# A mixture-of-experts decoder layer: the expert loop on TensorE flattened, weights split during the up projection, last token scatters with buffers of their own

## The chip, the cores and the metric

The kernel runs on one core of a Trainium2 chip, as one launch. The time is device microseconds of that core; less is better. The engines are named as in the profile: PE is TensorE (PEld its weight loads), ACT is ScalarE, DVE is VectorE, POOL is GpSimd, SP is SyncE, which only issues transfers.

## The reference, cut to what matters

A layer over 2 x 2048 rows of 512 numbers: linear attention, cross attention, and then a feed-forward part made of eight experts. The change touches the feed-forward part and the routing of the last rows before it.

```python
logits = x @ Wg.T                               # 4096 rows, 8 experts
top_v, top_i = jax.lax.top_k(logits, K)         # K = 2 experts a row
gates = jax.nn.softmax(top_v, axis=-1)
...
keep = pos_f < cap                              # cap = 1280 rows an expert
exp_batches = jnp.zeros((E, cap, d), x.dtype).at[flat_e, pos_safe].set(x[tok], mode='drop')
h = jnp.einsum('ecd,edf->ecf', exp_batches, W1)      # 512 -> 2 x 1024
inp, gate = jnp.split(h, 2, axis=-1)
h = jax.nn.gelu(inp, approximate=False) * gate
exp_out = jnp.einsum('eci,eid->ecd', h, W2)          # 1024 -> 512
out = jax.ops.segment_sum(contrib, tok, num_segments=N)   # each row: its experts' outputs times its gates
```

## The kernel before, in words

**Precision.** Every large product is made of three matmuls, because each operand is kept as a high part and a low part: high times high, high times low, low times high (`three`, L959 to L965; so one product shows as L963, L964 and L965 in a profile). ACT writes the high part (a copy that rounds), DVE subtracts it from the original and writes the low part (`low`, L1384).

**Before the experts.** The 4096 rows go through attention in eight groups of 512. For each group DVE finds the two experts of each row and their slots. POOL then writes row numbers and gates into a table in memory, eight indirect transfers a group (`scatter`, L600 to L607, shown as L605). `pack_tokens` (L1702) prepares the addresses `dest` and the words `pack` for them. Since there is one `dest` and one `pack`, DVE first waits until all scatters of the group before have landed (L1704). For the last group the row numbers are sent first, the gates later (`scatter_last_gates`, L608); DVE goes on with `cross_out` (L1661) only after `pack_tokens`. When all row numbers have landed, SP loads the first expert's part of the table (L472), POOL gathers the first four tiles of 128 rows (L651), and PE turns them (L1283).

**The experts.** Each of the eight has as many rows as were routed to it, known only at run time. They are worked off in chunks of four, four and two tiles (`CHUNKS`). A chunk is, on PE: `up`, eight jobs j of 24 matmuls over as many columns as there are rows (512, 384 or 256; L963 to L965 with output `pg`); two tiles of the next chunk turned (L1321, output `pt`); `out_tile(0)`, 24 matmuls (output `pj`); two more tiles turned when the next chunk has four; `out_tile(1)`; and tiles 2 and 3, or for tiles without rows an `empty_tile`, one matmul that only moves the counters on. PE's code is a loop over the experts around a loop over three chunks (L1287, L1293). At each expert it loads four numbers from the table `meta` into registers (L1288 to L1291), and chunks without rows are skipped by a branch (L1340).

For job j ACT makes the gelu (`gl`, L916), DVE multiplies with the other half (`hp`, L1808), ACT writes its high part (`hg_hi`, L919), DVE the low part (`hg_lo`). PE begins job j+2 when `hp` of job j is done, since `pg` has two banks for each half. The turned rows go from `pt` to `xe_hi` (ACT, L896) and `xe_lo` (DVE). An output tile is scaled by the gates on ACT into one of two buffers `ost` (L943) and added to the output by POOL with an indirect transfer (L682); each add waits for the one before to land.

**Weights.** An expert's weights come in twelve pieces of 512 KB, through four buffers `stage` (SP, L489): eight of the first matrix, four of the second. ACT copies a piece to its high part (`split`, L851, shown as L856), DVE writes the low part. The pieces of the second matrix are split within jobs 2 to 5 of the expert's first chunk. The eight pieces of the next expert's first matrix are split after the last chunk's `up`, on ACT between the output tiles (L935 to L938), on DVE after everything else (L1830 to L1832).

The order of all this is written out by hand; waits are on semaphores that count jobs, tiles and pieces.

## Time and profile before

| | |
|---|---|
| time, median of 3 runs | 1552.33 us (1551.38 to 1553.34) |
| the profiled execution's own time | 1546.13 us |
| its span, first to last instruction | 1544.3 us |
| PE busy | 1443.1 us, 93% of the span |
| DVE, ACT, POOL busy | 631.1, 586.0, 370.3 us |
| mean granted TensorE clock | 0.969 |
| PE's share of the chain that ended last | 80% |

A matmul's end is modelled: matmuls of 512 columns that start 0.23 us apart are shown as 0.39 us long each. So a stretch of PE is best read from the start of one instruction to the start of another. "Issue" as a releaser means that the engine waited for nothing that the profile shows: here register work and branches on its own sequencer.

### The profile page before, as it was taken

Reading aid. Unit: us, or ns where it says so; the run is one execution under the profiler, and the core shown is the slowest. Engines: PE = TensorE matmul, PEld = TensorE weight load, DVE = VectorE, ACT = ScalarE, POOL = GpSimd, SP = SyncE. Lnnn points to the kernel's source line nnn. Section 1 sums busy time; section 2 is a strip of 40 time slices with the busy share of each in tenths; the row PEclk is TensorE's granted clock in tenths of the full one; section 3 lists DMA queues with packets and bytes.
Section 4 is the critical chain, followed back from the end, with each engine's and each line's share of the span. In section 5 each row is a group of like instructions: output and inputs, shape, how many; then the busy total and the mean of one; then the engine's idle time right before and its main releaser. Section 6 shows DMA issues by size and latency. Waiting matters only on the chain.

```text
span 1544.3 us, 21052 instructions
## 1 busy us (share of the span) xinstructions
PE 1443.1 (93%) x7294; PEld 1208.9 (78%) x7295; DVE 631.1 (41%) x1410; ACT 586.0 (38%) x1001; POOL 370.3 (24%) x368
## 2 busy tenths in 40 slices
PE   6999999999983599999999899999999999999998
PEld 4768777778861487888888788898789888897886
DVE  6635666487775243311342431215441431214211
ACT  4535544367764142312332431234431422224211
POOL 3202222146765302011112112021112112021011
PEclk9999999999985699999999999999999999999999
DMA  9300220237655426221343432026523432035122
GB/s 204 56 0 28 82 110 28 82 102 200 164 120 144 124 79 165 60 34 21 96 143 54 129 89 41 7 48 190 148 83 54 113 104 41 0 54 150 14 41 27
DMA packets 80677, 132.46 MB, mean 86 GB/s; under 512 B 31954, under 2 KB 32082, under 8 KB 79604
## 3 DMA queue, kind: packets, MB, share of 16 engines
q1 hardware_dynamic: 63956, 97.67, 22.5%
q0 software_dynamic: 16672, 34.16, 12.0%
q8 instruction: 28, 0.46, 0.1%
q14 instruction: 21, 0.17, 0.0%
HBM read 93.90 MB, written 37.91 MB: 85 GB/s over the span
## 4 chain that ended last, share of the span: by engine, by line
PE 80%; POOL 4%; issue 4%; DVE 4%; DMA 4%; ACT 3%; ACTq 0%; SPq 0%; DVEq 0%; POOLq 0%
PE pg L963 16%; PE pg L965 15%; PE pg L964 15%; PE pj L963 8%; PE pj L965 8%; PE pj L964 8%; POOL slot_table L605 3%; PE pt L1321 1%; PE pj L1198 1%; DVE w_lo L1384 1%; DMA stage<-w 1%; DMA slot_table<-pack,dest 1%; PE pg L1226 1%; PE pg L1164 1%; DMA out_rows<-ost,etab 1%
## 5 line engine op out<-in xcount | busy, mean ns | idle before, releaser
L963 PE MATMUL pg<-xe_hi,w_hi 128*128 128x512 f32 (+2 forms) x1088 | 394.6, 363 | 21.9 <-issue 12.7
L965 PE MATMUL pg<-xe_hi,w_lo 128*128 128x512 f32 (+2 forms) x1088 | 393.3, 361 | 0.0
L964 PE MATMUL pg<-xe_lo,w_hi 128*128 128x512 f32 (+2 forms) x1088 | 393.2, 361 | 0.0
L1808 DVE TENSOR_TENSOR hp<-gl,pg 128x512 f32<-128x512 f32 (+1 forms) x136 | 87.1, 641 | 605.8 <-ACT gl L916 605.8
L682 POOL DMA_INDIRECT out_rows<-ost,etab x62 | 99.1, 1599 | 783.5 <-ACT ost L943 399.1
L963 PEld LDWEIGHTS pg<-xe_hi,w_hi 128*128 128x128 f32 x1088 | 207.8, 191 | 53.7 <-issue 14.2
L916 ACT ACTIVATE gl<-pg 128x512 f32<-128x512 f32 (+1 forms) x136 | 76.1, 560 | 456.3 <-PE pg L965 456.3
L965 PEld LDWEIGHTS pg<-xe_hi,w_lo 128*128 128x128 f32 x1088 | 207.7, 191 | 28.6
L964 PEld LDWEIGHTS pg<-xe_lo,w_hi 128*128 128x128 f32 x1088 | 207.9, 191 | 28.3
L963 PE MATMUL pj<-w_hi,hg_hi 128*128 128x512 f32 x464 | 183.4, 395 | 0.0
L965 PE MATMUL pj<-w_hi,hg_lo 128*128 128x512 f32 x464 | 180.8, 390 | 0.0
L964 PE MATMUL pj<-w_lo,hg_hi 128*128 128x512 f32 x464 | 180.7, 389 | 0.0
L1384 DVE TENSOR_TENSOR w_lo<-stage,w_hi 128x1024 fp32r<-128x1024 f32 x96 | 115.0, 1223 | 35.9 <-ACT w_hi L856 35.5
L943 ACT ACTIVATE ost<-pj,etab 128x512 f32<-128x512 f32 x62 | 42.6, 687 | 197.5 <-PE pj L965 186.8
L856 ACT ACTIVATE w_hi<-stage 128x1024 fp32r<-128x1024 f32 x96 | 99.0, 1057 | 40.0 <-DMA stage<-w 40.0
L965 PEld LDWEIGHTS pj<-w_hi,hg_lo 128*128 128x128 f32 x464 | 87.1, 188 | 18.3
L964 PEld LDWEIGHTS pj<-w_lo,hg_hi 128*128 128x128 f32 x464 | 87.2, 188 | 17.1
L963 PEld LDWEIGHTS pj<-w_hi,hg_hi 128*128 128x128 f32 x464 | 87.2, 188 | 17.1
L1384 DVE TENSOR_TENSOR hg_lo<-hp,hg_hi 128x512 fp32r<-128x512 f32 (+1 forms) x136 | 86.9, 639 | 1.9 <-ACT hg_hi L919 0.2
L919 ACT ACTIVATE hg_hi<-hp 128x512 fp32r<-128x512 f32 (+1 forms) x136 | 79.9, 587 | 4.1 <-DVE hp L1808 4.1
L605 POOL DMA_INDIRECT slot_table<-pack,dest x64 | 65.4, 1021 | 28.0 <-issue 17.2
L1384 DVE TENSOR_TENSOR xe_lo<-pt,xe_hi 128x512 fp32r<-128x512 f32 x66 | 42.6, 685 | 62.3 <-ACT xe_hi L896 62.1
(235 smaller groups left out, 1970.7 us busy)
## 6 DMA issues: line engine op xcount, KB each, us to landing
stage<-w SPq DMA_DIRECT2D x96, 512.0 KB, 5.0
xr<-x SPq DMA_DIRECT2D x8, 1024.0 KB, 10.0
out_rows<-xr SPq DMA_DIRECT2D x8, 1024.0 KB, 7.4
x_rows<-xn SPq DMA_DIRECT2D x8, 1024.0 KB, 7.4
x_in<-x SPq DMA_DIRECT2D x7, 1024.0 KB, 5.1
late_xT<-xT_hi SPq DMA_DIRECT2D x2, 1024.0 KB, 3.9
late_xT<-xT_lo SPq DMA_DIRECT2D x2, 1024.0 KB, 5.9
xT_hi<-late_xT SPq DMA_DIRECT2D x2, 1024.0 KB, 4.9
```

What stands on the lines that cost most here:

```text
L605: p.indirect_dma_start(out=to, out_offset=bass.IndirectOffsetOnAxis(ap=dest[:, c:c + 1], axis=0), in_=pack[:, c, 0:words], in_offset=None) ...
L682: p.indirect_dma_start(out=out, out_offset=bass.IndirectOffsetOnAxis(ap=etab[:, t, 0:1], axis=0), in_=ost[i % 2][:], in_offset=None, compu ...
L856: a.activation(w_dst(s), stage[s % STG][:], ACT.Copy).then_inc(s_w_hi, 1)
L916: a.activation(gl[j % 2][:, 0:w], pg[:, j % 2, 0:w], ACT.Gelu).then_inc(s_gl, 1)
L919: a.activation(hg_hi[:, j - 1, 0:w], hp[(j - 1) % 2][:, 0:w], ACT.Copy).then_inc(s_hghi, 1)
L943: a.activation(ost[i % 2][:], pj[i % 2][:], ACT.Copy, scale=etab[:, t, 1:2].bitcast(F32)).then_inc(s_yev, 1)
L963: nc.tensor.matmul(o, lh, rh, start=start, stop=False)
L964: nc.tensor.matmul(o, lh, rl, start=False, stop=False)
L965: return nc.tensor.matmul(o, ll, rh, start=False, stop=stop)
L1164: ins = mm(pg[:, 2 * (i % 2) + q // 2, (q % 2) * PW:(q % 2 + 1) * PW], qT[g % EARLY][:, q, i * P:(i + 1) * P], kv[g // NG][:, q, :], start ...
L1384: return v.tensor_tensor(dst, src, hi.bitcast(F32), ALU.subtract)
L1808: v.tensor_tensor(hp[j % 2][:, 0:w], gl[j % 2][:, 0:w], pg[:, 2 + j % 2, 0:w], ALU.mult).then_inc(s_hp, 1)
```

## The change

1. **PE.** One loop over 24 steps in place of the two loops. Six registers hold expert, chunk, rows left and three counters. The next values are worked out between `out_tile(0)` and `out_tile(1)`, with one load from `meta` for the next expert's count. Steps are not skipped in the middle; those left over come after the last chunk. An empty tile is now a matmul of 128 columns into `pg`, without a wait.
2. **ACT and DVE.** A loop over three chunks with one body in place of three written-out chunks. All operations are on 512 columns, also in chunks with fewer rows. Pieces of the second matrix are split in jobs 0 and 1 of an expert's first chunk, two each. The next expert's pieces are split in jobs 1 to 8 of its last chunk, one each, under an `If`.
3. **Output buffers.** Four `ost` in place of two; only tiles 0 and 1 wait for earlier adds.
4. **Last group.** `pack_last_tokens` writes `dest_tok` and `pack_last`, and waits for no scatter.

```diff
+            at_e, at_c, at_left, at_first, at_done, at_next = (
+                pe.alloc_register(f"pe_{n}") for n in ("expert", "chunk", "left", "first", "done", "count"))
...
-            with pe.Fori(0, EX) as e:
-                count = pe.value_load(meta[0:1, 0, bass.ds(e, 1)], min_val=0, max_val=CAP)
...
-                with pe.Fori(0, len(CHUNKS)) as c:
+            with pe.Fori(0, EX * len(CHUNKS)):
+                with pe.If(pe.snap(at_e, min_val=0, max_val=EX) < EX):
...
-                    def empty_tile(i):
-
-                        pe.wait_ge(s_yev, first + i)
-                        mm(pj[i % 2][:], w1_hi[:, 0, 0, 0:P], w2_hi[:, 0, :], start=True, stop=True).then_inc(s_y, 1)
+                    def empty_tiles(tiles):
+                        for i in tiles:
+                            mm(pg[:, 0, 0:P], hg_hi[:, 0, 0:P], w2_hi[:, 0, 0:P], start=True,
+                               stop=True).then_inc(s_y, 1)
...
+                    out_tile(0)
+                    pe.reg_load(at_next, meta[0:1, 0, bass.ds(e + 1, 1)])
...
+                    pe.reg_mov(at_left, (left - 4 * P) * more + coming * (more < 1))
+                    pe.reg_mov(at_e, e + (more < 1))
...
+                    out_tile(1)
```

ACT's new body (DVE's has the same frame, with `hp`, `hg_lo`, the low parts of pieces and `xe_lo`):

```diff
+                    weights_next = act.snap((left < 4 * P + 1) * (e < EX - 1), min_val=0, max_val=1)
...
+                        for j in range(FJ + 1):
+                            if j < FJ:
+                                act.wait_ge(s_h, done + (j + 1))
+                                if j >= 2:
+                                    act.wait_ge(s_hp, done + (j - 1))
+                                a.activation(gl[j % 2][:], pg[:, j % 2, :], ACT.Gelu).then_inc(s_gl, 1)
...
+                                a.activation(hg_hi[:, j - 1, :], hp[(j - 1) % 2][:], ACT.Copy).then_inc(s_hghi, 1)
+                            if j < 2:
+                                with act.If(c < 1):
+
+                                    act.wait_ge(s_y, first + 1)
+                                    for s in range(W1P + 2 * j, W1P + 2 * j + 2):
+                                        split(e, s)
+                            if j >= 1:
+                                with act.If(weights_next > 0):
+
+                                    split(e + 1, j - 1)
+                        evac(range(2))
+                        out_scaled(0)
+                        with act.If(next_is_full > 0):
+                            evac(range(2, 4))
+                        out_scaled(1)
+                        with act.If(c < 2):
+                            out_scaled(2)
+                            out_scaled(3)
```

The last group on DVE:

```diff
-                    pack_tokens(g)
+                    pack_last_tokens()
...
+            def pack_last_tokens():
+
+                link(v.tensor_tensor(slot[:], slot[:], trash[:], ALU.add))
+                flat = slot[:].rearrange("p i k -> p (i k)")
+                v.tensor_scalar(dest_tok[:], flat, 2.0, None, ALU.mult)
+                v.tensor_copy(pack_last[:, :, 0], tok[:].rearrange("p i k -> p (i k)")).then_inc(s_dest, 1)
```

PE before, at the head of the loop over the experts, ahead of the first `up` of an expert (ISA is a register operation):

```order
L1287 ISA
L1288 TENSOR_LOAD meta_125
L1288 ISA x2
L1289 ISA
L1289 TENSOR_LOAD meta_125
L1289 ISA x2
L1290 ISA
L1290 TENSOR_LOAD meta_125
L1290 ISA x2
L1291 ISA
L1291 TENSOR_LOAD meta_125
L1291 ISA x2
```

PE after: the head of its one loop, up to the first matmul of `up`.

```order
L1303 UNCONDITIONAL_BRANCH
L1304 COMPARE_AND_BRANCH
L1305 ISA
L1353 COMPARE_AND_BRANCH
L1315 ISA
L1317 ISA
L971 MATMUL pg<-xe_hi_206,w1_hi_196 128x512
```

PE after, between the last matmul of `out_tile(0)` and the first of `out_tile(1)`:

```order
L973 MATMUL pj0<-w2_hi_202,hg_lo_205 128x512
L1370 ISA
L1370 TENSOR_LOAD meta_127
L1372 COMPARE_AND_BRANCH
L1330 ISA
L1332 MATMUL pt0<-ident_49,xg_208 128x128 x4
L1330 REGISTER_ALU
L1332 MATMUL pt1<-ident_49,xg_208 128x128 x4
L1372 UNCONDITIONAL_BRANCH
L1374 ISA
L1376 ISA
L971 MATMUL pj1<-w2_hi_202,hg_hi_204 128x512
```

Four loads stood ahead of an expert's first matmul; now none does, and one load and the bookkeeping stand between the two output tiles of every chunk.

ACT before, after the last job of a third chunk: the high part of job 7, then the turned rows, then pieces.

```order
L919 ACTIVATE hg_hi_202<-hp1_210 128x256
L895 REGISTER_ALU
L896 ACTIVATE xe_hi_204<-pt0 128x4x128
L895 REGISTER_ALU
L896 ACTIVATE xe_hi_204<-pt1 128x4x128
L936 COMPARE_AND_BRANCH
L853 ISA
L856 ACTIVATE w1_hi_194<-stage0_196 128x1024
L856 ACTIVATE w1_hi_194<-stage1_197 128x1024
```

ACT after, job 7 and what follows it, for any chunk (the pieces only in an expert's last):

```order
L942 ACTIVATE gl1_210<-pg 128x512
L947 ACTIVATE hg_hi_204<-hp0_211 128x512
L955 COMPARE_AND_BRANCH
L857 ISA
L858 ACTIVATE w1_hi_196<-stage2_200 128x1024
L955 UNCONDITIONAL_BRANCH
L947 ACTIVATE hg_hi_204<-hp1_212 128x512
L955 COMPARE_AND_BRANCH
L857 ISA
L858 ACTIVATE w1_hi_196<-stage3_201 128x1024
L955 UNCONDITIONAL_BRANCH
```

The pieces have moved from behind the turned rows to ahead of them, one behind each job.

## Rows read from the trace of the kernel before

**Rows 1.** Windows: us, busy of PE, PEld, DVE, ACT, POOL; granted clock, DMA share, GB/s.
```profile
481.00:522.40 41.40, 6.25 (x19) 3.11 (x18) 15.67 (x41) 13.27 (x22) 19.14 (x22) 0.50 0.50 125
522.40:1536.30 1013.90, 994.54 (x4908) 849.84 (x4908) 307.84 (x422) 310.54 (x491) 165.35 (x134) 0.99 0.32 77
```
**Rows 2.** Waits of PE from 522 on: us in total, times, longest.
```profile
PE pg L963 <- issue: 12.7, 4, 5.1
PE pg L963 <- DVE w_lo L1384: 7.3, 4, 2.9
PE pg L963 <- DVE hp L1808: 1.9, 1, 1.9
```
**Rows 3.** Groups of PE by form from 522.3 on: busy, mean ns, idle before.
```profile
L963 PE MATMUL pg<-xe_hi,w_hi 128*128 128x512 f32 x704 | 279.1, 397 | 18.5 <-issue 12.7 <-DVE w_lo L1384 5.8
...
L963 PE MATMUL pj<-w_hi,hg_hi 128*128 128x512 f32 x464 | 183.4, 395 | 0.0
...
L963 PE MATMUL pg<-xe_hi,w_hi 128*128 128x256 f32 x256 | 72.5, 283 | 0.0
L963 PE MATMUL pg<-xe_hi,w_hi 128*128 128x384 f32 x128 | 43.0, 336 | 3.4 <-DVE hp L1808 1.9 <-DVE w_lo L1384 1.6
```
**Rows 4.** Windows of PE alone: one stretch each of `up` or output tiles.
```profile
663.68:707.21 43.53, 43.53 (x193) 1.00 0.10 21
708.00:729.86 21.86, 21.86 (x100) 1.00 0.25 30
729.86:752.89 23.03, 23.03 (x193) 1.00 0.29 65
1176.34:1209.65 33.31, 33.31 (x193) 1.00 0.18 42
522.40:568.64 46.24, 46.24 (x192) 0.94 0.38 115
594.88:640.14 45.26, 45.26 (x192) 0.96 0.34 91
876.89:923.35 46.46, 46.46 (x192) 0.94 0.44 125
```
**Rows 5.** Timeline of the last group's tokens: start, us, instruction, idle before.
```profile
488.41 0.17 DVE L1709 TENSOR_TENSOR slot<-slot,trash 128x8 f32<-128x8 f32 x1 [7.38 <-DMA slot_table<-pack,dest]
489.20 0.96 POOL L605 DMA_INDIRECT slot_table<-pack,dest  x1 [7.28 <-DVE pack L1713]
...
499.68 0.96 POOL L605 DMA_INDIRECT slot_table<-pack,dest  x1 [0.30 <-issue]
...
507.26 0.38 SPq L472 DMA_DIRECT2D etab_next<-slot_table  x1
```
**Rows 6.** Timeline of one job with a piece, and of the end of that `up`.
```profile
1073.82 0.60 ACT L916 ACTIVATE gl<-pg 128x512 f32<-128x512 f32 x1 [2.09 <-PE pg L965]
1074.84 1.06 ACT L856 ACTIVATE w_hi<-stage 128x1024 fp32r<-128x1024 f32 x1
1074.45 0.69 DVE L1808 TENSOR_TENSOR hp<-gl,pg 128x512 f32<-128x512 f32 x1 [1.47 <-ACT gl L916]
1075.92 1.23 DVE L1384 TENSOR_TENSOR w_lo<-stage,w_hi 128x1024 fp32r<-128x1024 f32 x1 [0.18 <-ACT w_hi L856]
1086.11 1.03 PE L1321 MATMUL pt<-ident,xg 128*128 128x128 f32 x8
1088.93 1.28 DVE L1384 TENSOR_TENSOR xe_lo<-pt,xe_hi 128x512 fp32r<-128x512 f32 x2
```
**Rows 7.** PE's sequencer, one line each: ns min/median/max, first and last start.
```profile
L1288 PEldq TENSOR_LOAD <-meta x8: 310/320/816, 518.3 to 1397.7; - x8
L1341 PEldq COMPARE_BRANCH  x28: 65/169/3335, 521.9 to 1508.9; - x28
```
**Rows 8.** ACT's waits from 522.4 on; landing of weight pieces from 600 on.
```profile
ACT L916 <- issue: 12.2, 8, 2.1
DMA to landing us min/median/max: 3.1/4.8/6.7
```

More of the change, by code:

```diff
@@ L256, in decoder @@
     hp = [ff(f"hp{i}", [P, GT]) for i in range(2)]
-    ost = [ff(f"ost{i}", [P, D]) for i in range(2)]
+    ost = [ff(f"ost{i}", [P, D]) for i in range(4)]
     assert base + ffn_at[0] <= nc.sbuf_usable_end, ffn_at
@@ L946, in _ @@
-                jobs(0)
-                with act.If(count > 4 * P):
-                    outs(0, False, CHUNKS[1])
-                    jobs(1)
-                    with act.If(count > 8 * P):
-                        outs(1, False, CHUNKS[2])
-                        jobs(2)
-                        outs(2, True, CHUNKS[0])
-                    with act.Else():
-                        outs(1, True, CHUNKS[0])
-                with act.Else():
-                    outs(0, True, CHUNKS[0])
+                three_chunks = act.value_load(meta[0:1, 3, bass.ds(e, 1)], min_val=0, max_val=1)
@@ new lines, in _ @@
+                    with pe.If(left > 3 * P):
+                        up(4)
+                    with pe.Else():
+                        with pe.If(left > 2 * P):
+                            up(3)
+                        with pe.Else():
+                            up(2)
+                    more = pe.snap(left > 4 * P, min_val=0, max_val=1)
+                    next_is_full = pe.snap((c % 2) * more < 1, min_val=0, max_val=1)
+                    gathered = pe.snap((first + (c < 2) * 2) * 16 + next_is_full * 32, min_val=32,
+                                       max_val=16 * (EX * ET + 16))
@@ L1361, in _ @@
+                    pe.reg_mov(at_e, e + (more < 1))
+                    pe.reg_mov(at_c, (c + 1) * more)
+                    pe.reg_mov(at_first, following)
+                    pe.reg_mov(at_done, done + FJ)
+                    out_tile(1)
+                    with pe.If(c < 2):
+                        with pe.If(left > 2 * P):
+                            out_tile(2)
                             with pe.If(left > 3 * P):
@@ L1363, in _ @@
                             with pe.Else():
-                                empty_tile(3)
+                                empty_tiles(range(3, 4))
+                        with pe.Else():
+                            empty_tiles(range(2, 4))
         @block.vector
```

212 lines of the change are left out of this document (93 added, 119 removed).

## The prediction

> **What bounds the kernel now.** I first read the windows by stage: from 522.4 to 1536.3 us, 1013.9 us long, PE does the experts and is busy for 994.5 us [rows 1]. So only what PE waits for, or does slowly, can be saved there, however much ACT and DVE gain. Ahead of it lie 41.4 us in which PE has 6.25 us of work at the low clock (0.50) while the last group is routed [rows 1].
>
> Second, the waits of PE [rows 2]. From 522 on it waits 12.7 us for "issue" in four places, 7.3 us for the low part of a weight piece in four, 1.9 us once for `hp`. One of the four "issue" waits is the start of the first expert; since the seven others for "issue" and `w_lo` are as many as there are changes of expert, I take the first matmul of each of the experts 1 to 7 to be what waits.
>
> Third, how long the stage takes without waits. The groups by form give the count: 704 matmuls of one line and 512 columns are 11 `up` of 64 each, 128 of 384 columns are 2, 256 of 256 columns are 4, and 464 are 58 output tiles of 8 [rows 3]. Undisturbed lengths are 43.53, 33.31 and 23.03 us for an `up` with 512, 384 and 256 columns, and 21.86 us for four output tiles, 5.465 each; between the end of one window at 707.21 and the next at 708.00 lie eight transposes, 0.79 [rows 4]. The sum is 11 x 43.53 + 2 x 33.31 + 4 x 23.03 + 58 x 5.465 + 34 x 0.79 = 478.8 + 66.6 + 92.1 + 317.0 + 26.9 = 981.4 us. Measured are 1013.9. So 32.5 us are lost.
>
> Where they go: the waits of rows 2, less some 3 us for the first start, are 18.7 us. After longer gaps the granted clock falls to the lower of its two levels for a few us: an `up` of 512 columns takes 45.26 after the first change and 46.46 at 876.89, with mean clock 0.96 and 0.94, against 43.53 at 1.00 [rows 4]. That is 1.7 and 2.9 us. Two more such gaps, by the waits of rows 2, I put at 1.7 each, so 8 us in all. The first `up` loses 46.24 - 43.53 = 2.7 us in the same way, after the 41 us of routing. The rest, 3 us, are the empty tiles and the part of each gap that the modelled ends of matmuls cover.
>
> **The change part by part.**
>
> *PE's loop.* Before, four loads from `meta` with their register operations stand ahead of an expert's first matmul. The first of them starts at 518.3 and the first matmul at 522.4; 1397.7 is the last [rows 7]. One load takes 0.32 us in the median, and with the operations around it I take 0.75, so 3 us for the four and over 4 with the loop's branches. All "issue" waits are this, less what PE still has queued. The `w_lo` waits are, I think, mostly this too, since ACT and DVE finish a piece at about the same time. Now six short instructions stand there, under 1 us. What is queued covers that: the one branch of 3.3 us in 28 [rows 7], within the first expert, is followed by no wait of PE in rows 2. Gain: the 18.7 - 1.9 us of gaps, the 8 us of low clock and 3 us of rest, 27.8, if the pieces are there.
>
> *Pieces during `up`.* They are: the first is split in job 1 of the last chunk, 20 us or more before the next expert. In this place the `w_lo` waits go whatever the register work was. The new cost is on ACT and DVE. One job with a piece keeps ACT from 1073.82 to 1074.84 + 1.06, 2.1 us, and DVE from 1074.45 to 1075.92 + 1.23, 2.7 us [rows 6]. A job of PE lasts 43.53 / 8 = 5.4, 4.2 or, in the narrow chunks, 2.9 us. So both keep up; DVE with only 0.2 us to spare in the four narrow ones, which are also charged the full 512 columns now. PE needs `hp` of job j one job later, and `hp` comes before the piece in DVE's order, so 0.2 us is not PE's margin; that is over 1 us. Cost 0.
>
> *The end of the last `up`.* Two pieces now stand ahead of `xe_lo` on DVE. Before, at the end of an `up` (PE turns at 1086.11), the two `xe_lo` end at 1088.93 + 1.28, 4.1 us later [rows 6]. Two pieces of 1.2 make that 6.5. PE wants it for the last four transposes after 0.79 + 5.47 + 0.4 = 6.65 us. Just in time, but then the bookkeeping (two register operations, some 0.3 us) is no longer covered. I take 0.5 us x 7 experts = 3.5; bounds 0 and 1.5 x 7 = 10.5, were DVE a further piece late.
>
> *The load and bookkeeping in each chunk.* Behind `out_tile(0)` a load of 0.3 to 0.8 us, in 17 chunks. 24 matmuls are queued or being queued there; cost 0, at most 0.8 x 17 = 13.6 if nothing covered it. I take 0.5.
>
> *One-chunk experts.* In their only chunk four pieces of the second matrix and eight of the next expert go through ACT, and the transfer of the next expert's first piece waits for the last adds and for a free buffer, then takes 4.8 us, 6.7 at most [rows 8]. ACT waits for it in job 1, in order, ahead of the next gelu. With jobs of 5.4 us it fits. With the 4.2 us of the expert at 1050 I expect up to 1 us; I take 0.5. The 1.9 us wait for `hp`, which is of this kind and in this expert, goes, since ACT is no longer held by pieces at the start.
>
> *Empty tiles and four output buffers.* The empty tile's wait for ACT is in the gaps already counted. ACT's waits for adds held no matmul but that.
>
> Stage of the experts: 27.8 + 1.9 - 3.5 - 0.5 - 0.5 = 25.2 us less.
>
> *Last group.* DVE waits 7.38 us for the scatters of group 6, and POOL 7.28 us for DVE; its usual spacing is 0.30 [rows 5]. With buffers of its own the wait is gone, and all behind it (scatters, the norm, `cross_out`, the store of the rows, the table load) moves up by 7.28 - 0.30 = 7.0 us. What comes last then? The last scatter is issued at 499.68, and the load that waits for its landing goes at 507.26 [rows 5]: over 6 us of landing under a megabyte of rows and two pieces of weights. These transfers move up with it, but now closer behind earlier ones. I take 6.5 us; bounds 7.2 and, if the table's writes are bound by transfers and not by DVE, 2. The low clock at the first `up` stays: PE still idles over 20 us.
>
> *Sum.* 25.2 + 6.5 = 31.7 us. The profiled execution, 1546.1 us, becomes 1514.4; the median of the runs lies 6.2 above it, so 1520.6.
>
> **A rule against this change.** There are over ten new conditional branches in every chunk on ACT and DVE. What the rows show of branches: 27 of 28 of L1341 take some 0.2 us or less, one takes 3.3, the first time it jumps far [rows 7]. The Trainium skill (Runtime: NRT & Kernel Launch, Instruction fetch mechanics) says that a taken branch to a target outside the code held on chip forces a fetch before anything goes on. By the rule each long jump would stall again and again; the trace agrees for the first jump and shows no second one, for PE. For ACT and DVE it is the slower rival below.
>
> **The rivals.**
> 1. *Late pieces (12%).* In the narrow last chunks a piece is wanted every 2.9 us. Four buffers and a cycle of 1.1 + 1.2 + 4.8 us allow one per 1.8; at a landing of 6.7 plus queueing behind gathers and adds, one per 3.5 or more. Then ACT waits in order ahead of gelu: 0.6 to 1 us x 8 jobs x 4 chunks = 20 to 30 us lost at worst, some 15 likely: 1535. For it: pieces do make ACT wait now. Against: four are loaded beforehand.
> 2. *The routing does not shorten (12%).* Scatters land late under the other transfers, gain 2 in place of 6.5: 1525.
> 3. *Register work not covered (10%).* After `out_tile(0)`, 0.8 us in each of 17 chunks, and 1.5 us at each last chunk: 13.6 + 7 more, 1541 at most, 1532 likely.
> 4. *Branches fetch code (4%), slower.* ACT's "issue" waits at the head of its expert loop are 12.2 us in 8, 1.5 each [rows 8]. If a taken branch cost that in each job, DVE's narrow jobs last 4.2 us in place of 2.9 (4 x 8 x 1.3 = 42 us) and each end of `up` is 1.5 to 3 us later (17 x 1.5 = 26): 68 us, 1588. It decides from some 0.6 us a branch on. Against: these waits hold several loads and a branch each.
>
> **How the numbers follow.** The forecast, 1520.6, has 62%; its own range is 1515 to 1528. The range of 8 in 10 reaches down to 1514, all costs at 0 and the full 7.2, and up into rivals 1 and 3, to 1533. A change of 0.2% (3 us) is about what the runs can tell. Only rival 4, or 1 and 3 together, come near no gain: faster 0.94, same 0.02, slower 0.04.
>
> **What would show it.** Right: PE's longest wait between experts under 0.5 us and none from `w_lo`; an `up` of 512 columns at 43.5 everywhere but in the first expert; the stage of experts at 986 to 991 us; the wait at DVE's slot addition gone and the first `up` at about 516. Wrong: narrow `up`s longer than 23.03; waits of `pt` for `xe_lo` over 1 us; ACT waiting for `stage` within `up`.

## The result: 38 us less, and more than was forecast

The changed kernel takes 1513.99 us in the median of its runs (1509.47 to 1517.61), the kernel before 1552.07 in the runs beside it. The ratio is 0.9749, with a 95% interval of 0.9731 to 0.9766. The forecast was 1520.6 us; its range began at 1514.0, and the median lies just below it.

The profiled execution took 1509.47 us with a span of 1507.8. Against the profiled execution of the kernel before this is 36.7 us less.

The windows of the changed kernel, cut at its first and last expert matmul, answer to [rows 1]. Columns as there.

```profile
477.00:516.64 39.64, 12.15 (x39) 5.67 (x40) 19.36 (x68) 13.48 (x23) 22.61 (x26) 0.50 0.66 160
516.64:1499.80 983.16, 983.16 (x4908) 843.67 (x4908) 319.50 (x422) 330.52 (x500) 168.13 (x135) 1.00 0.33 80
```

The experts take 983.2 us in place of 1013.9, so 30.7 less, and PE is busy in every one of them. The first `up` starts at 516.64 in place of 522.40, so 5.8 earlier. From the last matmul to the end it is 8.0 us in both. 30.7 + 5.8 + 0.2 outside the span are the 36.7.

PE's waits from 480 us on answer to [rows 2] (total, times, longest):

```profile
PE pt L1291 <- DMA xg<-x_rows,etab_next: 26.0, 4, 25.1
PE pg L971 <- issue: 1.5, 1, 1.5
```

Both lie ahead of the first expert matmul. Behind it none is left, where there were 18.7 us in eight (the 21.9 in nine of [rows 2] hold the start of the first expert, 3.2 us).

Groups of PE by form answer to [rows 3]: the work is the same, the idle time before it is 0.

```profile
L971 PE MATMUL pg<-xe_hi,w_hi 128*128 128x512 f32 x704 | 274.8, 390 | 1.5 <-issue 1.5
...
L971 PE MATMUL pg<-xe_hi,w_hi 128*128 128x256 f32 x256 | 72.4, 283 | 0.0
...
L971 PE MATMUL pg<-xe_hi,w_hi 128*128 128x384 f32 x128 | 42.8, 334 | 0.0
```

Windows of PE, one `up` each, answer to [rows 4]: the first, then one with 512 columns, one with 256, the first one behind a change of expert, and the one with 384 at the start of the expert that stood still for `hp` before.

```profile
516.64:561.74 45.10, 45.10 (x192) 0.97 0.55 180
585.37:628.90 43.53, 43.53 (x194) 1.00 0.29 82
718.65:741.69 23.04, 23.04 (x194) 1.00 0.64 170
754.36:797.88 43.52, 43.52 (x193) 1.00 0.27 79
1026.39:1059.70 33.31, 33.31 (x193) 1.00 0.57 182
```

The lengths are the undisturbed ones to 0.01 us, at the full clock (behind empty tiles an `up` of 512 columns takes 43.6). The narrow `up` of 23.04 us is one under which seven early pieces are split: it isn't longer. Only the first is, by 1.6 us.

The end of that narrow `up` in the timeline, PE and DVE, answers to [rows 6]:

```profile
741.69 1.03 PE L1332 MATMUL pt<-ident,xg 128*128 128x128 f32 x8
748.03 1.03 PE L1332 MATMUL pt<-ident,xg 128*128 128x128 f32 x8
```

```profile
743.98 1.22 DVE L1408 TENSOR_TENSOR w_lo<-stage,w_hi 128x1024 fp32r<-128x1024 f32 x1 [0.18 <-ACT w_hi L858]
745.13 0.68 DVE L1408 TENSOR_TENSOR hg_lo<-hp,hg_hi 128x512 fp32r<-128x512 f32 x1
745.73 1.22 DVE L1408 TENSOR_TENSOR w_lo<-stage,w_hi 128x1024 fp32r<-128x1024 f32 x1
746.86 1.28 DVE L1408 TENSOR_TENSOR xe_lo<-pt,xe_hi 128x512 fp32r<-128x512 f32 x2
```

PE turns the first pair at 741.69. `xe_lo` of both is done at 746.86 + 1.28 = 748.14, 6.45 us later. PE comes for the second pair at 748.03 and goes through it without a wait, because tile 2 needs only the first of the two, which is done 0.5 us before, and tile 3 comes a moment later: its first transpose starts 0.3 us after the second `xe_lo` is done.

The last group's tokens answer to [rows 5]: group 6's first scatter, then DVE's slot addition, the first and last scatter of the row numbers, the load of the table.

```profile
473.28 1.09 POOL L609 DMA_INDIRECT slot_table<-pack,dest  x1 [2.98 <-DVE pack L1747]
...
483.39 0.17 DVE L1739 TENSOR_TENSOR slot<-slot,trash 128x8 f32<-128x8 f32 x1
484.42 0.95 POOL L609 DMA_INDIRECT slot_table<-pack_last,dest_tok  x1 [0.30 <-issue]
...
494.90 0.96 POOL L609 DMA_INDIRECT slot_table<-pack_last,dest_tok  x1 [0.30 <-issue]
...
503.02 0.38 SPq L475 DMA_DIRECT2D etab_next<-slot_table  x1
```

The two waits of over 7 us are gone. In the kernel before, group 6's first scatter was at 471.10, so this execution came 2.2 us late to this place. Counted from it, the first `up` starts after 43.4 us in place of 51.3, which is 7.9 less.

ACT's waits from the first `up` on, of those in [rows 8]:

```profile
ACT ost L926 <- DMA out_rows<-ost,etab: 63.6, 14, 4.6
ACT L942 <- issue: 26.4, 8, 4.4
...
ACT w_hi L858 <- DMA stage<-w: 6.0, 6, 3.2
```

The waits for issue grew to 26.4 us from 12.2, and those for adds are 63.6 us. At the head of an expert ACT does register work: ahead of the gelu at 760.0, for one, four loads from `meta` of 0.27 to 0.28 us each stand with their operations from 755.4 to 757.8. All six waits for `stage` lie within an `up`, five in the first 20 us of the first one and one of 0.9 us in the expert that starts at 1026.4. None of it reaches PE.

### The profile page after: what moved, and what is told of

Its sections match the earlier page's. It is cut to its first block, busy times and chain, and to the rows that moved or that the text cites. A ratio compares the mean times of both kernels' runs of the same rounds, so it can differ in the third digit from the quotient of the medians.

```text
span 1507.8 us, 21734 instructions
## 1 busy us (share of the span) xinstructions
PE 1429.8 (95%) x7294; PEld 1201.5 (80%) x7295; DVE 643.3 (43%) x1410; ACT 605.5 (40%) x1010; POOL 372.4 (25%) x368
## 3 DMA queue, kind: packets, MB, share of 16 engines
q0 software_dynamic: 16672, 34.16, 12.4%
## 4 chain that ended last, share of the span: by engine, by line
PE 83%; POOL 4%; DMA 4%; DVE 3%; ACT 3%; issue 2%; SPq 0%; POOLq 0%; ACTq 0%; DVEq 0%
PE pg L971 16%; PE pg L973 16%; PE pg L972 16%; PE pj L971 9%; PE pj L973 9%; PE pj L972 9%; POOL slot_table L609 3%; PE pt L1332 2%; PE pj L1206 1%; DMA out_rows<-ost,etab 1%; PE pt L989 1%; DMA stage<-w 1%; PE pg L1172 1%; POOL qT L581 1%; PE pg L1234 1%
## 5 line engine op out<-in xcount | busy, mean ns | idle before, releaser
L971 PE MATMUL pg<-xe_hi,w_hi 128*128 128x512 f32 (+2 forms) x1088 | 390.0, 358 | 1.5 <-issue 1.5
L1844 DVE TENSOR_TENSOR hp<-gl,pg 128x512 f32<-128x512 f32 x136 | 93.5, 687 | 593.4 <-ACT gl L942 588.7
L942 ACT ACTIVATE gl<-pg 128x512 f32<-128x512 f32 x136 | 81.3, 598 | 375.9 <-PE pg L973 367.7
L1408 DVE TENSOR_TENSOR hg_lo<-hp,hg_hi 128x512 fp32r<-128x512 f32 x136 | 93.1, 685 | 1.0
L947 ACT ACTIVATE hg_hi<-hp 128x512 fp32r<-128x512 f32 x136 | 84.8, 624 | 2.3 <-DVE hp L1844 2.3
L609 POOL DMA_INDIRECT slot_table<-pack,dest x56 | 58.0, 1036 | 19.9 <-issue 15.2
## 6 DMA issues: line engine op xcount, KB each, us to landing
stage<-w SPq DMA_DIRECT2D x96, 512.0 KB
```

The costliest lines, as they stand in the source:

```text
L609: p.indirect_dma_start(out=to, out_offset=bass.IndirectOffsetOnAxis(ap=at[:, c:c + 1], axis=0), in_=words, in_offset=None).then_inc(s_scat ...
L942: a.activation(gl[j % 2][:], pg[:, j % 2, :], ACT.Gelu).then_inc(s_gl, 1)
L947: a.activation(hg_hi[:, j - 1, :], hp[(j - 1) % 2][:], ACT.Copy).then_inc(s_hghi, 1)
L971: nc.tensor.matmul(o, lh, rh, start=start, stop=False)
L1408: return v.tensor_tensor(dst, src, hi.bitcast(F32), ALU.subtract)
L1844: v.tensor_tensor(hp[j % 2][:], gl[j % 2][:], pg[:, 2 + j % 2, :], ALU.mult).then_inc(s_hp, 1)
```

## The experiments

Kernels of one round ran on one chip, with the kernel before beside them, and its median (in one round a single time) lay between 1544.6 and 1546.5 us there, 5.6 to 7.5 us lower than on the chip above. So I compare ratios, and apart from them the length of the experts' stage, which is read from one execution: from the first to the last expert matmul. It repeats well: the changed kernel has 983.2, 984.5, 983.8 and 983.9 us in four executions, while the start of the first `up` differs by 3 to 4 us between executions of the same kernel.

| kernel | time or ratio to the kernel before (95%) | experts' stage, us |
|---|---|---|
| last group alone | 0.9966 (0.9946 to 0.9987) | 1013.0 |
| PE's loop alone | 0.9880 (0.9863 to 0.9897) | 992.9 |
| ACT, DVE, four buffers alone | 0.9994 (0.9978 to 1.0010) | 1008.4 |
| changed kernel beside them | 0.9756 (0.9734 to 0.9777) | 984.5 |
| loads at the head, unused | one run, 1506.5 (before 1545.1) | 983.3 |
| loads in the middle, unused | one run, 1508.8 | 984.0 |
| one piece twice | one run, 1516.4 | 990.8 |
| two output buffers | one run, 1510.4 (before 1545.1) | 988.8 |
| four loads at the head | one run, 1528.9 (before 1545.7) | 1003.0 |
| five loads in the middle | one run, 1531.3 | 1005.5 |
| long filler | 0.9891 (0.9864 to 0.9918) | 992.6 |
| changed kernel beside it | 0.9767 (0.9738 to 0.9797) | 983.8 |
| short filler | 0.9769 (0.9746 to 0.9792) | 984.0 |
| changed kernel beside it | 0.9771 (0.9747 to 0.9795) | 983.9 |
| code moved | one run, 1518.3 (before 1546.5) | 991.8 |

### The parts one by one

**Last group alone.** The kernel before with `pack_last_tokens`:

```diff
-                    pack_tokens(g)
+                    pack_last_tokens()
```

> The kernel before with the fourth part of the change alone (own buffers for the last group's tokens). Theory A (the 7.0 us of waiting are the gain, transfers do not take any back): the first `up` starts 6.0 to 7.0 us earlier than 522.4, the four loads ahead of it and its low clock (46.2 us) stay, time 1552.1 - 6.5 = 1545.6, 1544.5 to 1546.5. Rival B (the table's writes are bound by transfers): gain 2, 1550.

Measured: the first `up` at 516.18, and 44.05 us after group 6's first scatter in place of 51.30. From that scatter to the last group's first one it takes 11.14 us in place of 18.10; in thirteen further executions with this edit it took 11.11 to 11.16. Theory A is right: the wait was worth 7.0, and nothing was taken back by the transfers: the landing behind the last scatter took 7.4 us, before 7.6. The ratio makes it 5.3 us of time, with an interval of 2 to 8.

**PE's loop alone.** ACT and DVE split the pieces where they did before, behind the turned rows.

```diff
-            with pe.Fori(0, EX) as e:
-                count = pe.value_load(meta[0:1, 0, bass.ds(e, 1)], min_val=0, max_val=CAP)
...
+            with pe.Fori(0, EX * len(CHUNKS)):
```

> The kernel before with TensorE's single loop and the new empty tiles alone; pieces are still split behind the turned rows and 522.4 us still stand ahead of the experts. Theory A (all gaps between experts, those put down to `w_lo` too, were register work): experts' stage 983 to 986 us from first to last `up` matmul start as in the changed kernel, no `w_lo` wait over 0.5 us, time 1552.1 - 31 = 1521, 1519 to 1524. Rival B (the `w_lo` waits were late pieces, so moving the pieces into `up` earned its share): four waits for `w_lo` of 1.5 to 3 us stay with 1.7 us of low clock behind each, 16 us saved at most, time 1534 to 1540.

Measured: ratio 0.988, 18.5 us, the stage 21.0 us shorter. Both theories are half wrong: A has the waits right, B is near the time. PE's waits behind the first `up`'s start in this kernel, one line in all:

```profile
PE pg L963 <- DVE hp L1824: 7.3, 4, 3.3
```

The pieces are split where they were before and PE comes sooner, yet there is no `w_lo` wait left: these were register work, as A says. But a wait that was not there before has come up: PE starts the new expert at once, does its first two jobs, and stands still for `hp` of job 0. DVE in the timeline around one such change of expert:

```profile
751.13 1.29 DVE L1400 TENSOR_TENSOR xe_lo<-pt,xe_hi 128x512 fp32r<-128x512 f32 x2 [4.57 <-ACT xe_hi L896]
752.33 4.62 DVE L1400 TENSOR_TENSOR w_lo<-stage,w_hi 128x1024 fp32r<-128x1024 f32 x4
...
762.49 2.46 DVE L1400 TENSOR_TENSOR w_lo<-stage,w_hi 128x1024 fp32r<-128x1024 f32 x2 [0.26 <-ACT w_hi L856]
767.23 1.28 DVE L1824 TENSOR_TENSOR hp<-gl,pg 128x512 f32<-128x512 f32 x2 [2.29 <-ACT gl L916]
```

The eight pieces keep DVE until 764.95 and ACT nearly as long, and only then come gelu and `hp` of job 0, which PE had ready at 761.4. Two windows of PE show what it costs, an `up` of 512 and one of 384 columns that should take 43.5 and 33.3 us:

```profile
755.97:800.79 44.82, 43.85 (x193) 1.00 0.52 168
1031.85:1070.27 38.42, 35.11 (x193) 0.96 0.61 195
```

In the second the clock fell too. Four such places make 10 us of the stage.

**ACT, DVE and four buffers alone.** PE's loops as before.

```diff
+                            if j >= 1:
+                                with act.If(weights_next > 0):
+
+                                    split(e + 1, j - 1)
```

> The kernel before with the loops of ScalarE and VectorE, the pieces within `up` and four output buffers alone; TensorE's loops as before. Theory A (register work is all): the gaps between experts stay at 1.5 to 5 us, all now put down to issue, time 1552.1 less 0 to 3 us, 1549 to 1552. Rival B (pieces were late): gaps halve, and 10 to 16 us go, 1536 to 1542. Rival C (branches or 512-column work on the other engines cost TensorE something that its own new loop hid): 1555 or more.

Measured: ratio 0.9994, no change that can be told, as theory A has it; the stage 5.5 us shorter. Of these 2.2 are at the expert whose `up` of 384 columns stood still for `hp` before (33.4 us in place of 35.6), 1.1 are a shorter low clock in the first `up` (45.1 us), and the rest is low clock behind gaps that stayed (one `up` of 43.6 us where it was 45.3, one of 45.7 where it was 46.5), so what the part itself earned is nearer to 2 us. PE's waits from the first `up`'s start on:

```profile
PE pg L969 <- issue: 20.1, 8, 5.5
PE pj L1344 <- ACT ost L924: 0.8, 1, 0.8
```

In [rows 2] 12.7 us were put down to issue and 7.3 to `w_lo`, 20.0 together in eight. Here, with every piece split well ahead, 20.1 in eight are all issue. So the `w_lo` waits named the wrong cause: the releaser that came last by the profile was DVE, but PE's sequencer was still at its registers.

**The changed kernel beside them.**

> The changed kernel once more, beside its parts: 1514, 1512 to 1517. If the parts add up (theory A: 6.5 + 31 + 0 = 37.5, less than 2 us from their meeting), it lies within 2 us of 1552.1 minus the sum of the three gains; if parts need each other (rival B), the three gains add up to 10 us less than its own.

The three gains are 5.3 + 18.5 + 0.9 = 24.7 us, its own is 37.7 us. Each of these is known to some 3 us, so the times speak for rival B: the parts need each other. The stage, which is less noisy, says that by 3 to 4 us they do: 21.0 + 5.5 = 26.5 us alone, 29.4 to 30.9 together. PE's loop uncovers 10 us of late pieces, and moving the pieces is worth little until it does. The other 9 of the 13 us are not found in the traces: the stage and the front of the parts alone (26.5, 7.0, and 1.5 from the four loads ahead of expert 0) make 35 us.

### The costs that I had charged

**One piece twice** (the eighth piece of an expert, into a scratch buffer first):

```diff
+                if again:
+                    low(scratch[:], stage[s % STG][:], hi)
                 low(lo, stage[s % STG][:], hi).then_inc(s_w_lo, 1)
```

> The changed kernel with the subtraction of an expert's eighth early piece done twice on VectorE (the first into a scratch buffer), which puts 1.1 to 1.2 us ahead of `xe_lo` at the end of each last `up`, 7 times. It measures the margin that I called just in time. Theory A (margin about 0.5 us, as 6.45 us from the turn to the end of the second `xe_lo` in the changed kernel's trace would have it): the second pair of turned tiles comes 0.5 to 0.9 us late in 7 chunks, 3.5 to 6.5 us more. Rival B (the margin is over 1.2 us): nothing. Rival C (none, and bookkeeping behind it uncovered): 1.2 to 2 us each, 8 to 14 us.

Measured: PE waits in seven places, one line in all from the first `up`'s start on; the stage is 990.8 us, 6.3 to 7.6 more.

```profile
PE pt L1333 <- DVE xe_lo L1409: 3.8, 7, 0.6
```

`out_tile(0)` and the second pair of turned tiles take 6.26 + 1.07 us there in place of 5.55 + 0.79, so 1.0 us in each place. From the first turn to the end of the second `xe_lo` it is 7.60 us in place of 6.45, so DVE was 1.15 us later. The margin is thus 0.15 us by this reckoning, 0.3 by the timeline above. The loss is just above A's 3.5 to 6.5 us, and "just in time" was right. The 0.5 us a place that I charged on top was not there in the changed kernel. Here it shows in part: where PE has to wait for `xe_lo`, the second pair takes 1.07 us in place of 0.79, so 0.3 us of bookkeeping behind it are no longer covered.

**Loads at the head and in the middle of a step, first attempt.**

```diff
+                    for _ in range(4):
+                        pe.reg_load(at_next, meta[0:1, 0, bass.ds(e + 1, 1)])
```

> The changed kernel with four extra loads from `meta` at the head of each chunk, ahead of `up`: the old register work put back, now in 17 chunks and with the pieces within `up`. Theory A (the sequencer's work costs only what exceeds the matmuls still queued): four loads of 0.3 to 0.75 us come on top of under 1 us, 2.3 to 4 us in all against a cover of 2.2 to 3.6, so gaps of 0 to 1.5 us at the start of `up`, 5 to 25 us in all over 17 chunks; all put down to issue, none to `w_lo`. Rival B (four loads alone are hidden; it was the nested loops and branches that made the gaps): no gap, no change. Rival C (nothing covers them): 17 x 3 = 50 us more.

> The changed kernel with four more loads behind `out_tile(0)` in each chunk, five in place of one. Theory A (24 matmuls and the turned tiles are queued there): no gap over 0.4 us between the output tiles, time unchanged within 2 us. Rival B (what I charged at up to 0.8 us a load is real and hidden by little): 1 to 3 us in each of 17 chunks, 17 to 50 us more.

Neither tells anything on these theories: nothing used the loaded values, and the traces have 17 + 1 loads of PE as in the changed kernel. They serve as two more executions of it, with stages of 983.3 and 984.0 us. So the loads were made live.

**Four loads at the head** (one behind `out_tile(0)` less):

```diff
+                    count = pe.value_load(meta[0:1, 0, bass.ds(e, 1)], min_val=0, max_val=CAP)
+                    tb = pe.value_load(meta[0:1, 1, bass.ds(e, 1)], min_val=0, max_val=EX * ET)
+                    ib = pe.value_load(meta[0:1, 2, bass.ds(e, 1)], min_val=0, max_val=EX * 3)
+                    three_chunks = pe.value_load(meta[0:1, 3, bass.ds(e, 1)], min_val=0, max_val=1)
+                    left = pe.snap(count - c * (4 * P), min_val=-8 * P, max_val=CAP)
```

> The changed kernel, but at the head of each step of its loop four numbers of the expert are loaded from `meta` and used (rows left, first tile, counter, three chunks), as the kernel before did once per expert; the load behind `out_tile(0)` is gone. In the first attempt at this, head_loads, nothing used the loaded values, no load is in its trace, and it tells nothing. Theory A (only what exceeds the queued matmuls costs): register work of 4 us against a cover of 2.2 to 3.6 leaves gaps of 1 to 2 us at 16 further starts of `up`, 16 to 32 us, and up to 1.7 us of low clock behind the longer ones: the experts' stage is 1005 to 1030 us in place of 983 to 984.5. Rival B (the two nested loops, not the loads, made the gaps): stage under 987. Rival C (nothing covers): 16 x 3.5 = 56, stage 1040.

Measured: the stage is 1003.0 us, 18.5 to 20 more, just below A. PE's only wait from the first `up`'s start on:

```profile
PE pg L971 <- issue: 15.5, 16, 1.5
```

**Five loads in the middle** (four live ones behind `out_tile(0)` more):

```diff
                     coming = pe.snap(at_next, min_val=0, max_val=CAP)
+                    tb = pe.value_load(meta[0:1, 1, bass.ds(e + 1, 1)], min_val=0, max_val=EX * ET)
+                    ib = pe.value_load(meta[0:1, 2, bass.ds(e + 1, 1)], min_val=0, max_val=EX * 3)
+                    none1 = pe.value_load(meta[0:1, 3, bass.ds(e, 1)], min_val=0, max_val=1)
+                    none2 = pe.value_load(meta[0:1, 3, bass.ds(e, 1)], min_val=0, max_val=1)
```

> The changed kernel with four more loads, whose values are used, behind the load that follows `out_tile(0)` in each chunk (in mid_loads they were unused and are not in its trace). Theory A (as at the head: the sequencer is some 2.2 us ahead of TensorE there, five loads with their operations take 4 us or more): a gap of 1 to 2 us before the turned tiles in 17 chunks, 17 to 35 us more, so that one load fits under the queue and five do not. Rival B (a whole output tile of 5.5 us covers them): time within 2 us of the changed kernel's, stage 983 to 985.

Measured: the stage is 1005.5 us, 21 to 22 more. A is right in the sum. PE's waits from the first `up`'s start on:

```profile
PE pt L1332 <- issue: 10.9, 14, 1.4
PE pj L971 <- ACT ost L926: 3.3, 3, 1.1
```

From start to start the loss is 1.9 us in the seven last chunks with an expert behind them (1.6 in the first of them), 1.4 in each of the three ahead of a narrow chunk, where no tiles are turned in between, and 0.6 in each of the others. PE in the timeline at one such place, and the operations of one of the five loads (ns min/median/max, first and last start):

```profile
1030.60 0.39 PE L973 MATMUL pj<-w_hi,hg_lo 128*128 128x512 f32 x1
1032.40 0.87 PE L1332 MATMUL pt<-ident,xg 128*128 128x128 f32 x6 [1.41 <-issue]
```

```profile
L1372 PEldq TENSOR_LOAD <-meta x17: 294/301/317, 566.9 to 1501.4; - x17
L1372 PEldq FUSED_REGOPS  x17: 159/159/159, 567.2 to 1501.7; - x17
L1372 PEldq SEQ_ASSERT  x17: 18/18/24, 567.5 to 1502.0; - x17
```

The load itself takes 0.30 us; with what stands around it the live ones follow each other every 0.7 to 0.8 us. Here the sequencer takes from 1028.8 to 1032.1, 3.3 us, for the five loads with their operations. Its first load begins 1.8 us before PE's last matmul of `out_tile(0)` starts. So about 2 us of sequencer work are covered at this place, one of those with the largest loss. One load and the bookkeeping fit under it, which is why they cost nothing in the changed kernel; by this reckoning, an estimate, about three loads are the limit.

**Two output buffers** in place of four:

```diff
-                        if i < 2:
-
-                            act.wait_ge(s_add, used if i == 0 else first * 16 + 16)
-                        a.activation(ost[i][:], pj[i % 2][:], ACT.Copy,
+                        act.wait_ge(s_add, used if i == 0 else first * 16 + 16 * i)
+                        a.activation(ost[i % 2][:], pj[i % 2][:], ACT.Copy,
```

> The changed kernel with two output buffers in place of four: ScalarE waits for an earlier add before each of the four scaled tiles. Theory A (the adds held no matmul): time unchanged within 2 us, ScalarE's waits for `out_rows` grow by 20 us or more, TensorE's do not. Rival B (with pieces in job 0 and 1 and gelus behind them, a late ScalarE reaches TensorE): waits of `pg` for `hp` or of `pj` for `ost` appear, 1 to 2 us in some of the four-tile chunks, 5 to 20 us more.

Measured in one execution: PE waits once for `hp`, 2.6 us, at the start of the fourth expert, behind a chunk with two tiles without rows. With the low clock behind it that `up` is long by 4.6 us (48.15 us from 853.81 on; the window holds the two empty tiles ahead of it too). ACT is what is late: it waits for an add until 860.43, and its first gelu of that `up` starts 12.4 us after the first matmul, in the changed kernel 6.3.

```profile
853.64:901.97 48.33, 45.70 (x196) 0.96 0.31 82
860.43 0.69 ACT L924 ACTIVATE ost<-pj,etab 128x512 f32<-128x512 f32 x1 [5.11 <-DMA out_rows<-ost,etab]
```

So B in one place, in one execution. Four buffers are worth up to 5 us there, in company with PE's new loop; I had put them at nothing.

### The low clock at the first `up`, and the code

**Long filler.** Matmuls without use on PE while it waits for the first rows:

```diff
+                pe.wait_ge(s_w_lo, 1)
+                filler(72)
+                pe.wait_ge(s_etab, 16)
+                filler(9)
                 for i in range(CHUNKS[0]):
+                    if i:
+                        filler(3)
                     pe.wait_ge(s_xg0[i], 16)
```

> The changed kernel with filler matmuls on TensorE (512 columns, results unused) while it waits for the first expert's rows: 72 after the last attention work, 9 after the table load has landed, 3 between the turned tiles, 4 behind them. It tests the term that I said stays, the low clock in the first `up` (45.1 us in place of 43.5, and 4.4 us of transposes at half speed). Theory A (the granted clock stays at 1.0 if TensorE is kept busy): first `up` 43.5 us, turned tiles 0.43 us each in place of 1.1, first `up` starts 0.3 to 0.7 us earlier, 2 to 3 us less in all: ratio to the changed kernel 0.998 to 0.9987. Rival B (the clock is granted by something other than TensorE's activity): first `up` 45 to 46.6 us, no gain. Rival C (fillers delay the turned tiles): first `up` starts later, slower by 1 to 3 us.

> The changed kernel again, on the chip and in the rounds of warm, to compare with it: about 0.9755 of the kernel before. Theory A has warm 2 to 3 us below it, theory B within 1 us, theory C above it.

Measured: slower than the changed kernel, ratio 0.9891 against 0.9767. Windows of PE: idle; the first nine fillers; the other 72; turned tiles; the first eight matmuls of `up`; the next.

```profile
482.00:491.60 9.60, 0.59 (x1) 0.50 0.68 163
491.60:495.60 4.00, 3.98 (x9) 0.50 0.78 167
495.60:512.00 16.40, 16.40 (x73) 1.00 0.57 153
512.00:519.20 7.20, 4.96 (x30) 1.00 0.02 0
522.93:526.40 3.47, 3.47 (x8) 0.51 1.01 368
526.40:530.00 3.60, 3.60 (x17) 1.00 0.76 212
```

PE was at 1.2 GHz when idle, went to 2.4 after nine fillers, and a tile's four transposes are shown as 0.60 us long in place of 1.09. But the fillers began only at 491.6, for `meta` isn't ready earlier, and ran until 512.0. The first rows had landed some 4.8 us before, if they took 3.4 us from their issue (503.8) as in the changed kernel. With 3.8 us from the last filler's start to the start of `up` (519.17 to 522.93) the clock was low again: `up` took 45.3 us. A's mechanism is there, and C's decides. ACT also took up some turned tiles 3 to 5 us after PE had them by the profile; why is open. And the stage is 8 to 9 us longer than in the changed kernel. Far behind the last filler PE waits 5.4 us for issue in five places, where the changed kernel has none.

**Short filler**: seven of them, behind the landing of the table load.

```diff
+                pe.wait_ge(s_w_lo, 1)
+                pe.wait_ge(s_etab, 16)
+                filler(7)
```

> The changed kernel with seven filler matmuls only, right behind the landing of the table load, so that they end with the landing of the first row gather (3.4 us later; a filler takes 0.43 us at the low clock in warm). In warm the clock was at 1.00 after nine fillers, but 81 of them held the turned rows up by 4.8 us. Theory A (the low clock at the first `up` can be had back by activity just ahead of it): four transposes of a tile take 0.35 to 0.5 us in place of 1.1, first `up` starts 0.5 to 0.8 us earlier after the first gather is issued, and lasts 43.5; 2 to 2.5 us less, ratio to the changed kernel 0.998 to 0.999. Rival B (seven fillers and transposes 1.4 us apart are too little): transposes at 1.1, first `up` 45 to 46.6 us, no change. Rival C (as in warm, a filler near the transposes delays what ScalarE sees of them): first `up` starts 1 us or more later.

> The changed kernel on the chip and in the rounds of warm_short. About 0.976 of the kernel before. Theory A has warm_short 2 us below it, theory B within 1 us, theory C above it.

Measured: 0.9769 against 0.9771, no difference. The clock stays at 0.50 through fillers, turned tiles and the start of `up`, which takes 46.1 us. Theory B. The 1.6 to 3.1 us of low clock at the first `up` stay.

**Code moved.** The 94 fillers of the long version in a branch that is never taken:

```diff
+            with pe.If(pe.snap(at_left, min_val=0, max_val=CAP) < 1):
+                pe.wait_ge(s_w_lo, 1)
+                filler(94)
```

> The changed kernel with 94 filler matmuls ahead of TensorE's loop in a branch that is never taken: the same code length as in warm, nothing of it carried out. In warm the experts' stage took 992.5 us in place of 983 to 984.5, with gaps of 3.4, 1.1, 0.9 and 1.0 us within chunks that no other run of the changed kernel has. Theory A (code that is moved in memory makes the loop fetch where it did not): such gaps appear here too, stage 988 to 993. Rival B (they came from the fillers themselves, by what ran late behind them): stage 983 to 985, and the far jump over the branch costs some 3 us once, ahead of the first `up`, at most.

Measured in one execution: the stage takes 991.8 us, theory A; the long version, with as much code ahead of the loop, has 992.6. PE's waits from the first `up` on, in a kernel that carries out the same instructions as the changed one but for one jump ahead of the loop:

```profile
PE pt L1340 <- issue: 3.3, 2, 2.8
PE pg L971 <- issue: 2.5, 3, 1.0
```

The branch in front of a chunk with 256 columns, in the changed kernel and in this one (ns min/median/max), shows where the three of `pg` are from:

```profile
L1356 PEldq COMPARE_BRANCH  x8: 65/188/342, 715.9 to 1327.2; - x8
```

```profile
L1364 PEldq COMPARE_BRANCH  x8: 65/258/3610, 720.4 to 1335.7; - x8
```

Three of the eight take 3.2 to 3.6 us here, in three different experts (starts 720.4, 824.4, 994.5), and cost PE 0.8 to 1.1 us each, 3 in all. The larger part has no branch in it. In the first expert PE stops in the middle of a tile's four transposes, and the clock is low behind it; from the first of these transposes to the end of `out_tile(0)` it takes 4.4 us longer than in the changed kernel. A second such stop, at 1067.65, costs 0.7 us.

```profile
561.96 0.43 PE L1340 MATMUL pt<-ident,xg 128*128 128x128 f32 x2
565.22 1.12 PE L1340 MATMUL pt<-ident,xg 128*128 128x128 f32 x4 [2.83 <-issue]
```

The queue of code in the profile (packets, MB) agrees, changed kernel first:

```profile
q8 instruction: 28, 0.46, 0.1%
```

```profile
q8 instruction: 34, 0.56, 0.2%
```

Six packets more, of 16 KB each. The Trainium skill (Runtime: NRT & Kernel Launch, Instruction fetch mechanics) says that code is held in blocks of 16 KiB, and that a taken branch out of the blocks at hand waits for a fetch. The trace agrees in size and in kind: a packet of 16,384 bytes starts 0.9 to 1.4 us into each of the three long branches. One also moves at 563.0, within the stop that has no branch. So my slower rival describes a thing that is there, on PE itself, and the changed kernel escapes it by where its loop happens to lie: 7 to 9 us hang on that.

## Why the forecast was 6.6 us too high

The mechanism was right in each of its large parts, and the sizes of the small ones were not. From the forecast of 1514.4 for the profiled execution to the 1509.5 measured it is 4.9 us (in favour 4.5 and 1.1 in the stage and 0.2 outside the span; against it 0.7 at the front; 0.1 or 0.2 is rounding):

- **Charges in the experts' stage: 4.5 us, measured 0.** These are the step that failed. The end of the last `up` (3.5), the load and bookkeeping (0.5) and the one-chunk experts (0.5) cost nothing: no wait of PE is left behind the first `up`. For the first, the time at which `xe_lo` ends was worked out rightly (6.5, measured 6.45), but then I charged 0.5 us for bookkeeping although by my own figures PE did not wait there. It doesn't, and the bookkeeping stays covered. `piece_doubled`, which makes PE wait, shows that the margin is 0.15 to 0.3 us and that 0.3 us of bookkeeping come uncovered only then; `mid_four` shows a cover of about 2 us. For the third, ACT does wait for a piece in that expert, 0.9 us where I had up to 1, and PE doesn't notice.
- **The first `up`: 1.1 us.** It took 45.1 us, in the kernel before 46.2. I had it stay at 2.7 us of low clock. It isn't the change but chance: executions of the changed kernel alone spread from 45.1 to 46.6.
- **The gaps: as worked out.** 27.8 and 1.9 us for waits, clock and rest were forecast, and with the two points above the 30.7 are accounted for to 0.1 us. Two errors in the sum behind it cancel, which is luck. There are 31 pairs of turned tiles (248 transposes in the trace), not 34, so I had 2.4 us too much; and an output tile beside turned tiles takes 5.54 to 5.58 us, not 5.465, so I had 2.1 too little, in both kernels. The 981.4 us came out right: with 1.6 us of low clock in the first `up` they are 983.0, and the stage is 983.2.
- **The front: forecast 6.5, measured 5.8, and 7.9 counted from group 6's first scatter.** The wait was worth 18.10 - 11.14 = 7.0, as worked out. The landing behind the last scatter took 8.1 us in place of 7.6, the half microsecond that I had set aside. What I left out is 1.5 us: the four loads ahead of the first expert stood between its last turned tile and its first matmul, and went with the others. From the first turned tile to `up` it takes 6.5 to 6.8 us in place of 8.3, in `pe_loop_only` too. What hides it here is that this execution came 2.2 us late to the front; in the executions of all kernels that scatter starts anywhere from 468.4 to 474.5.

The other 1.7 us are the step from the profiled execution to the median, which I took over from the kernel before as 6.2 us; it was 4.5.

**The `w_lo` waits** were read rightly as register work, and `act_dve_only` shows it. What I took from it was not complete. With PE's loop alone the low parts of the pieces come in time, but the pieces hold up the gelu and `hp` behind them, and that costs 10 us. I worked out both changes together and so missed nothing in the sum, but for PE's loop by itself my theory A had 31 us, and it was 18.5 by the ratio, 21 in the stage.

**The signs.** All that were to show the forecast right did, but the length of the stage: 986 to 991 us was expected, 983.2 measured. One that was to show it wrong came up too: ACT waits for `stage` within `up`, 6.0 us in six. It was a bad sign, for what counts is whether `hp` is late for PE, and it isn't.

**The rivals.** Late pieces (1): ACT's waits for them exist, but PE has none in the narrow `up`s. Routing that doesn't shorten (2): 7.0 of 7.0. Register work not covered (3): the estimate above puts the limit near three loads in that place, and there is one. Branches that fetch code (4): on ACT and DVE, where I feared them, they are short. From the first `up` on none of ACT's 260 takes over 0.05 us, and none of DVE's 243 over 0.07 but one of 0.7 us at 519.4. ACT's waits for issue at the heads are register work with loads. On PE one of 28 at the head of a step takes 3.6 us, within the first `up`, and is hidden (L1353, against L1341 in [rows 7]). But `code_moved` shows that the same loop in another place of memory pays for fetches on PE. So the rival missed the engine, and how much it costs hangs on something that no step of my prediction looked at.

**The range** ended at 1514.0 below, "all costs at 0 and the full 7.2". The costs were 0, and the lower end should have left room for what had no term of its own: the four loads ahead of expert 0 and the spread of the first `up`.

## What to carry to other kernels

When two engines' delays end at the same wait, taking one away pays only down to the next: here register work on PE and weight pieces on DVE lay over each other, and either alone gave 21.0 and 5.5 us of the 29.4 to 30.9 that both give. Before you charge an edit of a few hundred nanoseconds on a sequencer, count what is queued on its engine at that instruction; here about 2 us were, in the tightest places. And in a long loop with far branches, look at the longest run of each branch in the profile, and for stops of PE without one: this kernel loses 7 to 9 us if code that is never carried out stands in front of its loop.

## What was not expected of the hardware

- A load into a register costs PE's sequencer 0.30 us by itself and 0.7 to 0.8 with the operations that the program puts around it.
- When the loop lay 94 matmuls further on, three far branches more took 3.2 to 3.6 us, PE stopped once for 2.8 us in straight code, and six more code packets of 16 KB were moved.
- At 25 us of idling PE's clock was at 1.2 GHz; it rose to 2.4 in a run of back-to-back fillers, did not rise in a short run with the turned tiles and their gaps behind it, and was back at 1.2 behind 3.8 us from one matmul's start to the next.
- Values that nothing uses aren't loaded: an experiment with added loads has to use them, and its trace has to be searched for them.
